# A two-layer sandwich block on eight cores: the last LayerNorm's statistics gathered in the FFN loop, and the last stage cut into 512-column pieces on ScalarE, VectorE and two DMA queues

## The reference

```python
def reference(x, k_cache, v_cache, Wq, Wo, block_table, W0, b0, A, B):
    x = x + _layernorm(attn(_layernorm(x), ...))        # paged K/V, 32 heads of 128
    x = x + _layernorm(ffn(_layernorm(x), W0, b0, A, B))
    return x
# ffn: x @ W0.T + b0 + coef * sum_l mask_l * (x @ A_l.T @ B_l.T) / keep_l   (4 LoRAs of rank 16)
# _layernorm: (x - mean) / sqrt(var + 1e-5) over the last axis, 4096 wide
```

## Time and profile before

| what | value |
|---|---|
| three runs | 7086.5, 7299.5 and 7617.5 us, median 7299.5 |
| the profiled execution's own time | 7112.15 us |
| its span (slowest core, core 4) | 7110.6 us |
| spans of the eight cores | 7025.1 to 7110.6 us |
| TensorE matmul busy | 5204.4 us, 73% |
| VectorE busy | 1943.2 us, 27% |
| ScalarE busy | 1991.6 us, 28% |

### The profile page before, as it was taken

The page is one execution under the profiler, slowest core; times in us unless marked ns, Lnnn a source line. Parts: engine busy times, 40 slices in busy tenths (PEclk is TensorE's granted clock), DMA queues, the critical chain, the costliest instruction groups (busy, mean ns, idle before and its releaser), DMA issues.

```text
span 7110.6 us, 91739 instructions; the slowest of 8 cores (7025.1 to 7110.6 us)
## 1 busy us (share of the span) xinstructions
PE 5204.4 (73%) x35170; PEld 2773.3 (39%) x35776; DVE 1943.2 (27%) x3126; ACT 1991.6 (28%) x2193; POOL 106.9 (2%) x182
## 2 busy tenths in 40 slices
PE   2699996888788788878785878876114888888700
PEld 1344443555555555555552333332112333333300
DVE  6433332111111111111110000003775333333354
ACT  0000002878787787878780000000000000000000
POOL 0000000000000000000000000000000000000000
PEclk9799998999999999999997989987556989998855
DMA  4322222010101101010004131132333222223244
GB/s 154 81 59 54 63 54 51 13 25 15 26 16 25 25 16 25 16 25 13 19 13 128 40 62 40 40 62 71 127 124 103 58 56 59 58 58 69 71 177 171
DMA packets 147491, 420.21 MB, mean 59 GB/s; under 512 B 17136, under 2 KB 99584, under 8 KB 120192
## 3 DMA queue, kind: packets, MB, share of 16 engines
q0 software_dynamic: 21936, 135.29, 10.9%
q1 hardware_dynamic: 122832, 262.23, 10.4%
q10 hardware_dynamic: 2304, 16.78, 0.7%
HBM read 415.29 MB, written 117.44 MB: 75 GB/s over the span
## 4 chain that ended last, share of the span: by engine, by line
PE 55%; DVE 13%; DMA 13%; ACT 10%; issue 7%; SPq 1%; DVEq 0%; POOL 0%; ACTq 0%; PEldq 0%; POOLq 0%
PE qps L366 12%; PE wpso L562 12%; PE wpsf L562 10%; ACT BIGT L99 10%; PE cxb L113 9%; PE scps L91 9%; DVE stats L282 4%; DMA SS<-w 3%; DMA wslo<-wo 3%; DMA SS<-x 2%; DMA BIGT<-x2sp 2%; PE yps L581 1%; DVE xnb L295 1%; DVE x2b L662 1%; DVE SS L758 1%
## 5 line engine op out<-in xcount | busy, mean ns | idle before, releaser
L99 ACT ACTIVATE BIGT<-scps 128x1024 bf16<-128x1024 f32 x2048 | 1954.9, 1021 | 1537.3 <-PE scps L91 1532.1
L91 PE MATMUL scps<-qth,KT 128*128 128x512 bf16 x3748 | 1130.4, 389 | 177.7 <-ACT BIGT L99 141.6
L113 PEld LDWEIGHTS cxb<-SS,BIGT 128*128 128x128 bf16 x16384 | 1065.2, 99 | 277.9 <-issue 26.0
L113 PE MATMUL cxb<-SS,BIGT 128*128 128x129 bf16 x16384 | 1170.1, 223 | 0.6
L562 PE MATMUL wpso<-wslo,BIGT 128*128 128x512 bf16 x4014 | 928.0, 392 | 214.7 <-DMA wslo<-wo 125.0
L562 PE MATMUL wpsf<-SS,BIGT 128*128 128x512 bf16 x4002 | 957.8, 395 | 167.3 <-DMA SS<-w 160.9
L288 ACT ACTIVATE rstd<-aggr,epsb 128x1 f32<-128x1 f32 x64 | 18.9, 295 | 3369.4 <-DVE aggr L285 3369.4
L366 PE MATMUL qps<-BIGT,wqs 128*128 128x512 bf16 x4014 | 881.2, 379 | 23.4 <-DMA wqs<-wq 19.1
L562 PEld LDWEIGHTS wpso<-wslo,BIGT 128*128 128x128 bf16 x4096 | 408.0, 100 | 734.4 <-issue 278.7
L562 PEld LDWEIGHTS wpsf<-SS,BIGT 128*128 128x128 bf16 x4096 | 399.8, 101 | 716.3 <-issue 294.1
L127 DVE RECIPROCAL recb<-cxb 128x1 f32<-128x1 f32 x512 | 86.0, 168 | 1958.1 <-PE cxb L113 1901.6
(11 more groups left out here) (55 smaller groups left out, 1790.2 us busy)
## 6 DMA issues: line engine op xcount, KB each, us to landing
SS<-x SPq DMA_DIRECT2D x32, 2048.0 KB, 9.5
wqs<-wq POOLq DMA_DIRECT2D x32, 1024.0 KB, 8.0
wslo<-wo POOLq DMA_DIRECT2D x32, 1024.0 KB, 21.1
SS<-w POOLq DMA_DIRECT2D x32, 1024.0 KB, 19.2
out<-SS SPq DMA_DIRECT2D x16, 2048.0 KB, 7.3
mtb<-m SPq DMA_DIRECT2D x384, 64.0 KB, 2.2
qsp<-qst SPq DMA_DIRECT2D x32, 512.0 KB, 2.6
qth<-qsp SPq DMA_DIRECT2D x32, 512.0 KB, 3.2
```

Of the source, the lines that this page charges most:

```text
L91: last = nc.tensor.matmul(c.scps[pk][:, no:no + nw], c.KT[kv % 2][:, kt * 128:(kt + 1) * 128], c.qth[parh][:, th * c.TH + no: th * c.TH + ...
L99: nc.scalar.activation(E[:, kt * c.TH:(kt + 1) * c.TH], c.scps[pk], AF.Exp, scale=SCALE), "expd")
L113: last = nc.tensor.matmul(c.cxb[bk][:, slot * 129:slot * 129 + 129], E[:, kt * c.TH + tc * 128: kt * c.TH + (tc + 1) * 128], c.vp[(kv % 2) ...
```

## The change

Three things change.

First, in the FFN every finished 512-column tile `ostf` also gets a `bn_stats` on VectorE, right behind the addition that makes it, with a wait of VectorE on that addition. The statistics go to `stats_f`, 768 float32 columns in PSUM, six for each (tc, os_). In the last slice (os_ = 7) a `bn_aggr` follows for each token tile and puts mean and variance into `aggT` in SBUF.

Second, the last stage no longer takes statistics. ScalarE makes Ln and Exp of the tile's stored variance, VectorE makes -mean*rstd in one 128x1 operation (`nmrb`), and the normalisation becomes eight ScalarE activations (Identity with a per-partition scale and bias) of 512 columns into one float32 buffer `obuf`. VectorE adds `x2t` to each piece in place, and each piece is stored by a DMA of its own, the first four from SP's queue, the last four from ScalarE's.

Third, the buffers: two slots for the loads in place of four, one `obuf` for the results in place of two, and a semaphore for each of the eight pieces. The activation of a piece waits until the store of that piece of the tile before has landed.

```diff
                             vv = S.inc(nc.vector.tensor_tensor(ost[pw], accb,
                                                                wps[pw], ALU.add),
                                        "comb")
+                            if stat_buf is not None:
+                                S.wait(nc.vector, "comb", vv)
+                                vs = S.inc(nc.vector.bn_stats(
+                                    stat_buf[:, tc * 48 + os_ * 6:
+                                             tc * 48 + os_ * 6 + 6], ost[pw]),
+                                    stat_sem)
+                                if os_ == nos - 1:
+                                    S.wait(nc.vector, stat_sem, vs)
+                                    S.inc(nc.vector.bn_aggr(
+                                        agg_buf[:, 2 * tc:2 * tc + 2],
+                                        stat_buf[:, tc * 48:(tc + 1) * 48]),
+                                        stat_sem)
...
             for tc in range(NTC):
...
-                S.wait(nc.vector, xsem, v1)
-                if tc >= 2:
-                    S.wait(nc.vector, "fina" if par == 0 else "finb",
-                           (tc // 2) * 16)
-                rl = ln_tile(ft, outb[par])
-                S.wait(nc.vector, "lnd", rl)
-                lnd_fin[tc] = S.inc(
-                    nc.vector.tensor_tensor(outb[par], outb[par], x2t, ALU.add),
+                slot_free = p7base + NCH * (tc - 1)
                 if tc >= 2:
+                    S.wait(nc.scalar, "p7v", slot_free)
+                vft = S.inc(nc.scalar.dma_start(
+                    ft, ffnsp[tc * 128:(tc + 1) * 128, :]), fsem, 16)
+                if tc >= 2:
+                    S.wait(nc.sync, "p7v", slot_free)
+                vx2 = S.inc(nc.sync.dma_start(
+                    x2t, x2sp[tc * 128:(tc + 1) * 128, :]), xsem, 16)
...
+                S.wait(nc.scalar, fsem, vft)
+                S.wait(nc.vector, xsem, vx2)
+                for k in range(NCH):
+                    if tc >= 1:
+                        S.wait(nc.scalar, bsem[k], bbase[bsem[k]] + 16 * tc)
+                    vact = S.inc(nc.scalar.activation(
+                        p7ps[k], ft[:, k * 512:(k + 1) * 512], AF.Identity,
+                        bias=nmrb[:, p:p + 1],
+                        scale=rsf[:, 2 * p + 1:2 * p + 2]), "sself")
+                    S.wait(nc.vector, "sself", vact)
+                    vaf = S.inc(nc.vector.tensor_tensor(
+                        p7ps[k], p7ps[k],
+                        x2t[:, k * 512:(k + 1) * 512], ALU.add), "p7v")
+                    S.wait(qeng[k], "p7v", vaf)
+                    S.inc(qeng[k].dma_start(
+                        out_d[tc * 128:(tc + 1) * 128, k * 512:(k + 1) * 512],
+                        p7ps[k]), bsem[k], 16)
```

More of the change, by code:

```diff
@@ L252, in build_program @@
         epsb = nc.alloc_sbuf_tensor("epsb", [128, 1], F32).ap()
+        aggT = nc.alloc_sbuf_tensor("aggT", [128, 2 * (NT // 128)], F32).ap()
         barv = [0]
@@ L611, in out_proj @@
                                        + (it // 2) * 16)
-                            S.inc(nc.vector.tensor_copy(ost[pw], wps[pw]), "woev")
+                            ve = S.inc(nc.vector.tensor_copy(ost[pw], wps[pw]),
+                                       "woev")
+                            if stat_buf is not None:
+                                S.wait(nc.vector, "woev", ve)
+                                vs = S.inc(nc.vector.bn_stats(
+                                    stat_buf[:, tc * 48 + os_ * 6:
+                                             tc * 48 + os_ * 6 + 6], ost[pw]),
+                                    stat_sem)
+                                if os_ == nos - 1:
+                                    S.wait(nc.vector, stat_sem, vs)
+                                    S.inc(nc.vector.bn_aggr(
+                                        agg_buf[:, 2 * tc:2 * tc + 2],
+                                        stat_buf[:, tc * 48:(tc + 1) * 48]),
+                                        stat_sem)
                         if lora:
@@ L720, in build_program @@
                          yps=[yps0_g.ap(), yps1_g.ap(), yps2_g.ap(), yps3_g.ap()],
-                         wsl_ap=SS.bitcast(BF16))
+                         wsl_ap=SS.bitcast(BF16),
+                         stat_buf=stats_f_g.ap(), stat_sem="fstat",
+                         agg_buf=aggT)
         barrier()
@@ L725, in build_program @@
             p7 = contextlib.ExitStack()
[L726 to L734, removed]
@@ L763, in build_program @@
-            S.wait(nc.sync, "fina", S.val("fina"))
-            S.wait(nc.sync, "finb", S.val("finb"))
+            SSB7 = SS.bitcast(BF16)
+            fts = [SSB7[:, 0:D], SSB7[:, D:2 * D]]
+            x2s = [SSB7[:, 2 * D:3 * D], SSB7[:, 3 * D:4 * D]]
+            rsf = p7.enter_context(nc.sbuf_tensor("rsf", [128, 4], F32)).ap()
+            nmrb = p7.enter_context(nc.sbuf_tensor("nmrb", [128, 2], F32)).ap()
+            obuf = p7.enter_context(nc.sbuf_tensor("obuf", [128, D], F32)).ap()
+            p7ps = [obuf[:, k * 512:(k + 1) * 512] for k in range(8)]
@@ new lines, in build_program @@
+            bsem = ["fina", "qspa", "ctxsta", "wosta",
+                    "finb", "qspb", "ctxstb", "wostb"]
+            qeng = [nc.sync] * 4 + [nc.scalar] * 4
+            bbase = {s: S.val(s) for s in bsem}
+            p7base = S.val("p7v")
+            NCH = D // 512
+            ln_val, nm_val, ex_val = {}, {}, {}
+            for tc in range(NTC):
+                p = tc % 2
+                ft, x2t = fts[p], x2s[p]
+                fsem = "xlda" if p == 0 else "xldb"
+                xsem = "xldc" if p == 0 else "xldd"
+                slot_free = p7base + NCH * (tc - 1)
+                if tc >= 2:
+                    S.wait(nc.scalar, "p7v", slot_free)
[5 more added lines that the diff above has]
+                    x2t, x2sp[tc * 128:(tc + 1) * 128, :]), xsem, 16)
+                if tc >= 2:
+                    S.wait(nc.scalar, "p7v", slot_free)
+                S.wait(nc.scalar, "sself", S.val("sself"))
+                ln_val[tc] = S.inc(nc.scalar.activation(
+                    rsf[:, 2 * p:2 * p + 1], aggT[:, 2 * tc + 1:2 * tc + 2],
+                    AF.Ln, bias=epsb), "sself")
+                S.wait(nc.scalar, "sself", ln_val[tc])
+                ex_val[tc] = S.inc(nc.scalar.activation(
+                    rsf[:, 2 * p + 1:2 * p + 2], rsf[:, 2 * p:2 * p + 1],
+                    AF.Exp, scale=-0.5), "lnd")
+                S.wait(nc.vector, "lnd", ex_val[tc])
+                if tc >= 2:
+                    S.wait(nc.vector, "p7v", slot_free)
+                nm_val[tc] = S.inc(nc.vector.tensor_scalar(
+                    nmrb[:, p:p + 1], aggT[:, 2 * tc:2 * tc + 1],
+                    rsf[:, 2 * p + 1:2 * p + 2], -1.0, ALU.mult, ALU.mult),
+                    "lnd")
+                S.wait(nc.scalar, "lnd", nm_val[tc])
+                S.wait(nc.scalar, fsem, vft)
[15 more added lines that the diff above has]
+                        p7ps[k]), bsem[k], 16)
@@ L765, in build_program @@
+            for s in bsem:
+                S.wait(nc.sync, s, S.val(s))
             p7.close()
```

24 lines of the change are left out of this document (4 added, 20 removed).

## The result

The change makes the kernel a little faster, by less than the two per cent that the prediction takes as the limit between the same and faster: the ratio to before is 0.9883 with a 95% interval of 0.9848 to 0.9918. The profiled execution takes 7009.52 us against 7112.15. The medians of ten runs each are 7168.0 us (7007.5 to 7575.2) and 7309.9 us (7086.5 to 7617.5); runs in which one die or both show a lower TensorE clock pull both medians up, and the ratio leaves them out.

The account below looks back on a forecast made before the run. Mostly TensorE's chain bounds the kernel; the last stage is a chain of waits. Its 8.0 + 188.2 + 85.5 + 2.6 + 4.4 = 288.7 us against 382.7 saves 94, giving 7018 us; range 6960 to 7205.

Parts of the forecast that it names:

- The compute part: Last stage, per tile: five activations at 0.80 us plus late-piece finishes and rounds, 11.76 us in all.
- The load part: Last stage, per tile: the next ffnsp load, issued behind piece 7 and not fetched ahead, 5.70 us.
- the rest of the store just ahead: Last stage: delay of the ffnsp load by the last quarter MB stored, at 2.2 us a MB, 0.55 us.
- rival 1: Last stage: the ffnsp load meets the stores and takes 9.3 us; tile 21.3 us, total 7076 us; chance 0.14.
- The ends of the stage: Last stage: first loads 8.0 us; at the end, last store's landing 2.6 and closing waits 4.4 us.
- 7112 - 94 = 7018 us: Whole kernel: profiled execution less the last stage's gain of 94 us, FFN taken as 0; 0.987 of before.
- the 7203 that I gave only as an end of the range: Whole kernel: 0.987 of the 7299.5 us median of before; the stated range reached to it, ending at 7205.
- The FFN's price of 128 us: FFN: rival that the statistics hold TensorE up in every turn, 128 us, total 7146 us; chance 0.05.
- All steps are short: Last stage: rival that all low ends hold, total 6977 us or a few us below; chance 0.16.
- The paragraph on VectorE and ScalarE: Last stage: pieces made on VectorE would take 7.9 us instead of 11.76, some 60 us less over sixteen tiles.
- 1.34 us a piece: Last stage, pieces from 4 on: hand-over, VectorE's addition and store issue before ScalarE's next activation, 1.34 us each.
- the old wait: Last stage before: VectorE waits some 10 us a tile for the x2sp load queued behind a store, 164.6 us in all.

Follow-up runs that it names:

- the first run with both together: Kernel before with statistics moved to the FFN, one Ln and Exp for all tiles, 4096-wide VectorE work, loads two tiles ahead; stage 208 to 218 us.

## Why the prediction was right or wrong

**The mechanism and the ratio were right.** 0.987 was forecast and 0.9883 measured. The stage was to take 288.7 us and took 291.9 on the slowest core, the tile 17.5 and 17.8. The additions waited for no x2sp load and no activation for a store, on any core; and TensorE waited for VectorE's addition 0 to 11 us in the FFN, by core, as it did before (0 to 10).

**The sizes, term by term.** The activation takes 0.805 us, as worked out (0.80), but five in a row cost 3.63 and not 4.00, since neighbours overlap by 0.1. The round of a late piece takes 2.12 us, against 2.14. The compute part is 11.23 us (6742.77 to 6754.00, the last store being issued at 6753.66 for 0.34) against 11.76. The load part was under-sized by somewhat more: 17.8 - 11.2 = 6.6 us against 5.70. The step that failed there is "the rest of the store just ahead", a quarter MB at 2.2 us a MB: the load lands in 6.8 us (6.2 to 7.0 by core, so at the very edge of the 7 that I had named as a sign against) and not in 5.45, since not one but about two stores were in flight, each held up by the x2sp load (4.5 us, not 2.6). It is rival 1 in part, 0.9 us a tile where rival 1 had 3.85. The ends of the stage were off as well: 9.0 us and not 8.0 for the first loads, and 5.2 us from the issue of the last store to the end of the span (7002.79 to 7008.0) where the sum has 2.6 and 4.4. These errors nearly cancel, so that 288.7 came so near to 291.9 is in part luck.

**The absolute time was wrong.** The step that failed is the sum, "7112 - 94 = 7018 us", which takes the stage's gain off the profiled execution and not off the median of before. It holds for executions like the profiled one, 7009.52 us, and four of the ten runs of the change take 7007 to 7030. But the stated value stood beside a median of 7299.5, against which it reads as a gain of 281 us or 4%, while my working says 94 us or 1.3%, and the runs show 1.2%. The median came out at 7168.0, 150 us above the stated value. The number that followed from the working for it was the 7203 that I gave only as an end of the range.

**Rivals.** The FFN's price of 128 us did not come: both statistics instructions stand in the gap of 3.63 us, 1.3 us of it in the turn shown, and 2.69 us of waiting for the masks are left. "All steps are short" did not come either. The paragraph on VectorE and ScalarE found a real cost but at the wrong place. By the estimate there, arithmetic on VectorE would have made the pieces 60 us cheaper; no run tried them so. The kernel that does the work on VectorE, in one piece, is only 10 us shorter, and its rows show it waiting 10.5 us a tile for the x2sp load behind the store. What the change gives away is in ScalarE's queue: the stores there, behind VectorE's additions, cost 57 us, which the line that moves them to SP's queue gets back. I had those waits in the sum as 1.34 us a piece, but did not ask what the tile would be without them.

**What the old wait was.** I read it rightly as the queue's order and not as bandwidth: with the loads ahead VectorE waits for none of them behind the first tile. The prediction did not follow this to its end, that the order alone is worth more than the change, nor did it ask what the moved statistics bring without the pieces: 97 us of the stage, 10 more than with them.

## What to carry to other kernels

When a stage's chain is load, compute, store, look first at what stands ahead of the next load in its queue; loads two tiles ahead brought 148 us of the stage here, and taking the statistics off the engine that waited brought 97. Don't put a DMA that waits for another engine into the queue of an engine that has work of its own behind it. When an edit shortens compute, ask which transfers it pushes together: the same bytes issued within 0.6 us cost 2.1 us a tile more than with one of the loads under the compute. And state an absolute time in the frame of the number it will be compared with.

## What was not expected of the hardware

Cores 4 and 5 took 370 us for the stage in which the other six took 320. The queue rows of core 4 and then core 5, for the kernel with the moved statistics alone:

```profile
6884.39 0.34 SPq L803 DMA_DIRECT2D out<-SS  x1
...
6907.79 0.34 SPq L803 DMA_DIRECT2D out<-SS  x1
```

```profile
6884.47 0.34 SPq L803 DMA_DIRECT2D out<-SS  x1
...
6907.72 0.34 SPq L803 DMA_DIRECT2D out<-SS  x1
```

Each counts from its own start, and by that the two issue their 4 MB within 0.1 us of each other, tile after tile, 23.3 us apart; the x2sp load lands in 15.5 us there. Cores 0 and 1 stand 7.8 us apart (6889.13 and 6896.90), and it lands in 11.9. In the change the stages come in pairs on six cores: 299.5 and 297.1 us on cores 0 and 1, 291.8 and 291.9 on 4 and 5, 290.1 and 289.2 on 6 and 7; cores 2 and 3 fit less well (299.8 and 295.5). That neighbours share memory bandwidth and fall into or out of step would explain the 370 us; the Trainium skill, "DMA: Bandwidth & Descriptors", Specifications, gives some 358 GB/s as a core's half of what two cores share. The most seen here over 150 us is 334 (core 4 of the first run with both together); slices of 5.8 us reach 372 (core 6 of the run with all stores on SP's queue), and what the neighbour moved in them was not read, so no run here tests the share. No run shifted one core against its neighbour, so the cause stays argued and not shown.

With their output in PSUM the statistics take 0.70 us (the row of L610 above), where the prediction had 0.61 to 0.68 from those into SBUF: none of the factor of two that it allowed was needed.
